# Layer 1 in another order on all five engines, attention values in 64x32 tiles, the last tile in halves of 256 columns, one masking pass moved

## The chip, the cores and the metric

The kernel runs on one core of a Trainium2 chip. A core has TensorE (matrix products into PSUM), VectorE, ScalarE, GpSimd and a DMA queue on SyncE; each takes its instructions in order, and they wait for each other by semaphores. All data are 32-bit floats. The metric is the device time of one execution in microseconds (us), lower is better. An fp32 matmul shows as two instructions in the trace, so 16 matmuls are 32 rows there.

## What is computed

A stack of two layers over x, 64 sequences of 32 rows with 512 columns. Layer 0 is a cross-attention over a context, self-attention and a linear layer with adapters. The change lies in layer 1 and in the gates ahead of it:

```python
# layer 1 of the reference, shortened
x = x + gates(layernorm(x), conv_w, gamma, beta)   # crucial and other channels, each scaled by a sigmoid gate
# attention: 8 heads of 32 columns, 32 rows per sequence, softmax over rows
q, k, v = split(layernorm(x) @ w_qkv.T + b_qkv)
scores = where(causal, k_h @ q_h.T, -10000.0)
attn = softmax(scores)
x = x + (attn @ v_h) @ w_o.T + b_o
x = x + layernorm(x) @ (W * mask).T
```

The gates need means and variances over all of x, so layer 1 can't begin before they are known.

## The kernel before

x lies in SBUF as 16 tiles (NT) of 128 rows (four sequences) by 512 columns, `x_tile(t)`. Four tiles are in flight; tile t uses lane u = t % 4 of the buffers and of PSUM, where `low(u)` and `high(u)` are two banks of 512 columns. Each tile goes through some 30 stages in layer 1. On TensorE: `turn_mix` (four 128x128 transposes of the gated features), `turn1` (of the normalised rows), `qkv` (16 matmuls of 128 columns for q and k, 4 of 256 for v), `scores`, `values`, `project`, `turn2`, `ffn` (4 matmuls of 512 columns). On ScalarE: `xnT1` and `xnT2` (copies of the turned rows), `evac_qk`, `exps`, `spread_p`, `evac_ot`. On GpSimd: `rstd1` and `rstd2` (the reciprocal root), `bias`, `spread_k`, `shift`. On VectorE: `gate`, `add_rest`, `mix`, `add_mix`, `stats1`, `rows1`, `evac_v`, `mask`, `turn_probs`, `add_proj`, `stats2`, `rows2`, `add_ffn`. On SyncE: `store`.

The order is set by numbers. `SLOTS1` gives each stage a place in the life of a tile, and `STARTS1` gives each of the first eight and the last four tiles its start. `over_lanes` sorts the stages of an engine by slot plus start; tiles in the middle follow in a loop, one tile per unit of the slots. Single entries can be overridden by `OPENING1` and `CLOSING1`. Before, TensorE and VectorE used `OPENING1`, ScalarE alone used `CLOSING1`. An engine never leaves its order: a stage that waits holds all behind it.

`values` computes for each of 8 heads the product of 128x32 of V with 128x128 of the spread probabilities. A tile holds four sequences, and each sequence attends only to itself, so `spread_p` writes the turned probabilities four times, each time with the rows of three sequences set to zero by a column of `jmask`.

In the gates, VectorE also multiplies the weights of the last product with their mask, in four passes (`mask_weights`, 128x512 each), between the short steps of the statistics. `keep_busy` issues matmuls on a constant that nothing reads: 13 stand ahead of the first `turn1`, 2 ahead of the projection of tile 14 and 7 ahead of the values of tile 15.

Of the kernel before, what the change touches and what calls it, by code (L numbers as in the profile page):

```python
# [64 lines left out]
def build_program(nc, a):  # L65
    ctx = ExitStack()
    with ctx:
# [3 lines left out]
        def sem(name):  # L71
# [12 lines left out]
            ("jmask", [P, TB]),  # L84
# [1106 lines left out]
def norm_turn(pe, n, t, u, xn, out, ident):  # L1191
    pe.wait_ge(n["xn"], t + 1)
    for c in range(DC):
# [16 lines left out]
    "gate": 0.000, "add_rest": 0.027, "mix": 0.173, "turn_mix": 0.485, "add_mix": 0.614, "stats1": 0.707,  # L1210
    "rstd1": 0.773, "rows1": 0.929, "bias": 2.020, "turn1": 1.011, "xnT1": 1.045, "qkv": 1.310,
    "evac_qk": 1.500, "evac_v": 1.762, "spread_k": 1.600, "scores": 2.006, "mask": 2.056, "shift": 2.136,
    "exps": 2.342, "turn_probs": 2.461, "spread_p": 2.571, "values": 2.919, "evac_ot": 2.919,
    "project": 3.015, "add_proj": 3.074, "stats2": 3.162, "rstd2": 3.245, "rows2": 3.395, "turn2": 3.470,
    "xnT2": 3.539, "ffn": 3.877, "add_ffn": 3.989, "store": 3.989,}
# [3 lines left out]
STARTS1 = ((0.00, 0.45, 0.99, 1.56, 3.50, 4.58, 5.35, 6.53),  # L1219
           (0.00, 37.47, 38.83, 39.38))  # L1220
# [3 lines left out]
OPENING1 = {("add_rest", 1): 0.715, ("mix", 1): 0.935, ("turn_mix", 1): 1.012}  # L1224
CLOSING1 = {("evac_ot", NT - 2): 41.65}
# [383 lines left out]
def mix_gates(nc, ctx, neghalf, ps, Y, ones, blend, band, affine, late, late_in, reduced):  # L1609
# [70 lines left out]
    def dve_program(dve):  # L1680
# [20 lines left out]
        mask_weights(2)  # L1701
# [18 lines left out]
def layer1(nc, ctx, a, X, mask, ident, neghalf, x_tile, ps, bufs, blend, early, late, late_in, ones, blended):  # L1720
# [32 lines left out]

    def sp_program(sp):
        def store(t, u):
            sp.wait_ge(s["ffn_added"], t + 1)
# [8 lines left out]
    def pool_program(pool):
# [308 lines left out]
```

## Time and profile before

| | |
|---|---|
| median of 3 runs | 2002.39 us (2001.21 to 2002.53) |
| the profiled execution, its own time | 2003.22 us |
| its span | 2001.3 us |
| layer 1 on TensorE, first turn to last matmul | 1761.37 to 1998.12 |
| TensorE, VectorE, ScalarE, GpSimd busy | 98%, 67%, 40%, 44% of the span |

Times in the rows count from the start of the span. A row of the timeline gives the start, the time from the first start to the last end of a group of like instructions, the engine (PE TensorE, DVE VectorE, ACT ScalarE, POOL GpSimd), the line, the tile written and the tiles read, and in brackets the idle time ahead of it and what ended it. The end of a matmul is modelled and takes in its drain, so successive groups on PE overlap a little: how long a stage holds TensorE is read from one start to the next.

### The profile page before, as it was taken

Reading aid. Unit: us, or ns where it says so; the run is one execution under the profiler, and the core shown is the slowest. Engines: PE = TensorE matmul, PEld = TensorE weight load, DVE = VectorE, ACT = ScalarE, POOL = GpSimd, SP = SyncE. Lnnn points to the kernel's source line nnn. Section 1 sums busy time; section 2 is a strip of 40 time slices with the busy share of each in tenths; the row PEclk is TensorE's granted clock in tenths of the full one; section 3 lists DMA queues with packets and bytes.
Section 4 is the critical chain, followed back from the end, with each engine's and each line's share of the span. In section 5 each row is a group of like instructions: output and inputs, shape, how many; then the busy total and the mean of one; then the engine's idle time right before and its main releaser. Section 6 shows DMA issues by size and latency. Waiting matters only on the chain. (4 is left out here: it accounts for less than half of the span.)

```text
span 2001.3 us, 41730 instructions
## 1 busy us (share of the span) xinstructions
PE 1963.2 (98%) x13298; PEld 1607.5 (80%) x13298; DVE 1332.3 (67%) x4426; ACT 802.4 (40%) x2285; POOL 883.1 (44%) x1506
## 2 busy tenths in 40 slices
PE   9999999999999999999999999999899999898998
PEld 7989889898988889898988989898665665575675
DVE  5846648483755748375574848466678888667875
ACT  3434435353444435344443544444333333232332
POOL 5543545354454536345453634446233333233442
PEclk9999999999999999999999999999999999999999
DMA  7100001010100101010010101010300000000000
GB/s 287 55 26 28 21 26 32 26 32 15 35 23 26 32 15 42 15 33 25 26 32 15 32 26 32 25 29 1 124 1 1 1 1 0 32 1 22 22 16 27
DMA packets 28323, 62.98 MB, mean 31 GB/s; under 512 B 14465, under 2 KB 15681, under 8 KB 27298
## 3 DMA queue, kind: packets, MB, share of 16 engines
q1 hardware_dynamic: 28194, 61.61, 9.4%
q8 instruction: 39, 0.64, 0.1%
q14 instruction: 90, 0.74, 0.1%
HBM read 54.15 MB, written 4.29 MB: 29 GB/s over the span
## 5 line engine op out<-in xcount | busy, mean ns | idle before, releaser
L792 ACT ACTIVATE probs<-psLane,nmax 128x289 f32<-128x289 f32 x256 | 126.7, 500 | 476.7 <-DVE nmax L914 476.7
L954 DVE MAX8 top<-work 128x8 f32<-128x257 f32 x512 | 180.1, 414 | 2.7
L492 PEld LDWEIGHTS psLane<-posT,lanes 128*128 128x128 f32 x1536 | 177.3, 192 | 4.8 <-ACT QT L781 0.6
L492 PE MATMUL psLane<-posT,lanes 128*128 128x128 f32 x1536 | 179.4, 275 | 0.4 <-ACT QT L781 0.4
L939 DVE TENSOR_TENSOR X<-X,psLane 128x512 f32 (+1 forms) x15 | 10.3, 687 | 242.0 <-PE psLane L1067 242.0
L1067 PE MATMUL psLane<-posT 128*128 128x512 f32 x384 | 167.7, 592 | 0.4 <-PEq L105 0.4
L767 ACT ACTIVATE w_o<-psLane 128x384 f32<-128x384 f32 (+1 forms) x256 | 113.9, 453 | 89.4 <-PE psLane L545 88.5
L345 POOL TENSOR_TENSOR tails<-probs,unit 128x66 f32<-128x66 f32 x128 | 38.1, 298 | 251.6 <-ACT probs L792 251.0
L565 PE MATMUL psLane<-KT,QT 96*128 96x289 f32 x512 | 146.0, 406 | 0.0
L1067 PEld LDWEIGHTS psLane<-posT 128*128 128x128 f32 x384 | 72.4, 190 | 84.9 <-issue 84.9
L370 POOL TENSOR_TENSOR KT<-w_qkv 128x128 f32<-128x128 f32 x64 | 29.2, 457 | 251.3 <-ACT w_qkv L739 251.3
L911 DVE TENSOR_REDUCE rmax<-psLane 128x2 f32<-128x578 f32 x128 | 97.0, 758 | 46.7 <-PE psLane L565 46.6
L515 PE MATMUL psLane<-hid,lanes 128*128 128x256 f32 x512 | 122.7, 381 | 0.0
L1173 POOL TENSOR_TENSOR lane_rstd<-lane_veps,neghalf 128x1 f32<-128x1 f32 x79 | 49.7, 629 | 161.8 <-DVE lane_veps L1168 161.8
L781 ACT ACTIVATE QT<-psLane 96x512 f32<-96x512 f32 x96 | 56.9, 593 | 131.9 <-PE psLane L492 131.3
L565 PEld LDWEIGHTS psLane<-KT,QT 96*128 96x128 f32 x512 | 91.2, 191 | 21.2 <-issue 7.2
L934 DVE COPY posT<-psLane 128x384 f32<-128x384 f32 x64 | 34.9, 545 | 104.4 <-PE psLane L621 104.4
L545 PE MATMUL psLane<-WvT,hid 128*128 128x192 f32 x512 | 104.2, 326 | 0.0
L545 PE MATMUL psLane<-w_ffn 128*128 128x192 f32 x512 | 104.1, 326 | 0.0
L958 DVE MATCH_REPLACE8 work<-top,work 128x257 f32<-128x257 f32 x256 | 102.3, 414 | 0.0
L958 DVE MATCH_REPLACE8 work<-top_last,work 128x257 f32<-128x257 f32 x256 | 102.2, 412 | 0.0
L958 DVE MATCH_REPLACE8 work<-top,hid 128x257 f32<-128x257 f32 x256 | 101.9, 408 | 0.0
(242 smaller groups left out, 5099.9 us busy)
## 6 DMA issues: line engine op xcount, KB each, us to landing
hid<-in_ctxT SPq DMA_DIRECT2D x64, 514.0 KB, 3.5
y<-X SPq DMA_DIRECT2D x16, 256.0 KB, 2.0
X<-in_x SPq DMA_DIRECT2D x1, 3584.0 KB, 21.1
lanes<-in_WqT SPq DMA_DIRECT2D x4, 768.0 KB, 9.6
Vtail<-Vlat SPq DMA_DIRECT2D x128, 24.0 KB
posT<-in_WoT SPq DMA_DIRECT2D x1, 3072.0 KB, 13.0
w_qkv<-in_w_qkv SPq DMA_DIRECT2D x2, 1536.0 KB, 6.9
w_ffn<-in_w_ffn SPq DMA_DIRECT2D x2, 1024.0 KB, 6.9
```

Source lines behind the costliest of these rows:

```text
L492: mm = pe.matmul(out[:, P * r:P * r + P], WqT[:, c, w:w + P], xnT[:, c, :], start=(c == 0), stop=(c == DC - 1))
L515: mm = pe.matmul(out[:, 0:MAIN], WkT[:, c, 2 * P:3 * P], hid[:, j, c, 0:MAIN], start=(c == 0), stop=(c == DC - 1))
L545: mm = pe.matmul(out, left(c), right(c), start=(c == 0), stop=(c == 1))
L565: mm = pe.matmul(psS[:, g % 2, 0:S], QT[:, g, j, :], KT[0:HD, j % 2, g, :], start=True, stop=True)
L767: act.activation(vproducts[:, 2 * f:2 * f + n, :].rearrange("p a n -> p (a n)"), psKV[:, kv_bank(t, 7 * j + 3 + f), 0:VH * n], ACT.Copy).t ...
L781: ins = act.activation(QT[at:at + hi - lo, g].rearrange("p j (r q) -> p r j q", r=G), src[lo:hi], ACT.Copy)
L792: act.activation(probs[:, g, :], psS[:, g % 2, 0:S], ACT.Exp, bias=nmax[:, g:g + 1], scale=XSCALE, accum_out=rsum[:, j % 2, g:g + 1]).then ...
L911: dve.tensor_reduce(rmax[:, 2 * h:2 * h + 2], psS[:, :, 0:S], AX.X, ALU.max).then_inc(rmax_done, 1)
L954: ins = dve.max(top[step // 2][:, c, :], src[:, c, :] if step == 1 else work[:, c, :])
L958: ins = dve.match_replace(work[:, c, :], picked[:, c, :], src[:, c, :] if step == 2 else work[:, c, :], GONE)
L1067: mm = pe.matmul(out, OT[:, n // G, n % G].rearrange("p j q -> p (j q)"), WoT[:, n, :], start=(n == 0), stop=(n == NKT * G - 1))
L1173: pool.tensor_tensor(small["rstd"][:, u], small["veps"][:, u], neghalf[:], ALU.pow).then_inc(n["rstd"], 1)
```

## The change

All numbers of `SLOTS1` and `STARTS1` are new, `OPENING1` grows from 3 entries to 24 and `CLOSING1` from 1 to 12, and all five engines now use both. `values` works on sequences in pairs: the two row halves of the array hold two sequences each, a matmul is 64 rows by 32 columns with 64 columns moving, and 16 of them replace 8; `spread_p` then writes two copies instead of four, with two new columns of `jmask`. For the last tile `xnT2`, `ffn`, `add_ffn` and `store` work on halves of 256 columns. In the gates `mask_weights(2)` stands ahead of the wait for the first sums instead of behind `moment`.

```diff
@@ SLOTS1, STARTS1, OPENING1, CLOSING1
-    "gate": 0.000, "add_rest": 0.027, "mix": 0.173, "turn_mix": 0.485, "add_mix": 0.614, "stats1": 0.707,
...
+    "gate": 0.0000, "add_rest": 0.3412, "mix": 0.4805, "add_mix": 0.5579, "stats1": 0.5919, "turn_mix": 0.7364,
...
-STARTS1 = ((0.00, 0.45, 0.99, 1.56, 3.50, 4.58, 5.35, 6.53),
-           (0.00, 37.47, 38.83, 39.38))
+STARTS1 = ((0.0000, 0.5197, 0.9241, 1.5710, 3.6120, 4.4460, 5.1756, 6.5717),
+           (0.0000, 34.2135, 38.2969, 38.6761))
@@ mix_gates, dve_program
+        mask_weights(2)
         dve.wait_ge(sums_done, 1)
         dve.tensor_scalar(minus_mean[:], sums, 1.0, None, ALU.mult).then_inc(mean_ready, 1)
         mask_weights(1)
         dve.wait_ge(sums_done, 2)
         dve.tensor_scalar(moment[:], sums2, -1.0, EPS, ALU.mult, ALU.add).then_inc(moment_ready, 1)
-        mask_weights(2)
@@ layer1
-    pT = lambda u: lanes[:, u, 1]
+    pT = lambda u: lanes[:, u, 1, 0:2 * EW].rearrange("p (h k q) -> p h k q", h=EH, k=2)
+    last_tile = lambda t: isinstance(t, int) and t == NT - 1
@@ store
+            if last_tile(t):
+                for n in range(2):
+                    sp.wait_ge(s["ffn_added"], t + 1 + n)
+                    sp.dma_start(a["y"][t][:, EW * n:EW * n + EW], x_tile(t)[:, EW * n:EW * n + EW]).then_inc(out_done, 16)
@@ every engine, here POOL
-        over_lanes(pool, SLOTS1, STARTS1, {
+        over_lanes(pool, SLOTS1, STARTS1, opening_slots=OPENING1, closing_slots=CLOSING1, stages={
@@ values
-            for h in range(EH):
-                n, at = h // 4, L * (h % 4)
-                mm = pe.matmul(high(u)[at:at + L, P * n:P * n + P], V[:, u, L * h:L * h + L],
-                               pT(u)[:, P * h:P * h + P], start=True, stop=True, tile_position=(0, at))
+            for n in range(2):
+                for c in range(EH // 2):
+                    for half in range(2):
+                        h, lo, at = 4 * n + c, 64 * half, 512 * half + 2 * L * n
+                        mm = pe.matmul(ps[L * c:L * c + L, u, at:at + 2 * L], V[lo:lo + 64, u, L * h:L * h + L],
+                                       pT(u)[lo:lo + 64, h].rearrange("p k q -> p (k q)"), start=True, stop=True,
+                                       tile_position=(lo, L * c))
@@ ffn
+            if last_tile(t):
+                for n, out in enumerate((low(u)[:, 0:EW], high(u)[:, 0:EW])):
+                    for c in range(DC):
+                        if (n, c) == (0, 2):
+                            pe.wait_ge(n5["xnT"], t + 2)
+                        mm = pe.matmul(out, xnT[:, u, c], w_ffn[:, c, EW * n:EW * n + EW], start=(c == 0), stop=(c == DC - 1))
+                    mm.then_inc(s["ffn_filled"], 1)
+                return
@@ spread_p
-            for j in range(TB):
-                ins = act.activation(pT(u).rearrange("p (h j q) -> p h j q", h=EH, j=TB)[:, :, j], v, ACT.Copy,
-                                     scale=jmask[:, j:j + 1])
+            for k in range(2):
+                ins = act.activation(pT(u)[:, :, k], v, ACT.Copy, scale=jmask[:, TB + k:TB + k + 1])
@@ xnT2 of the last tile
+            for n in range(2):
+                act.activation(xnT[:, u, 2 * n:2 * n + 2].rearrange("p c q -> p (c q)"), high(u)[:, EW * n:EW * n + EW],
+                               ACT.Copy).then_inc(n5["xnT"], 1)
@@ add_ffn
+            if last_tile(t):
+                for n, part in enumerate((low(u)[:, 0:EW], high(u)[:, 0:EW])):
+                    dve.wait_ge(s["ffn_filled"], t + 1 + n)
+                    half = x_tile(t)[:, EW * n:EW * n + EW]
+                    dve.tensor_tensor(half, half, part, ALU.add).then_inc(s["ffn_added"], 1)
+                return
```

TensorE's order, with names of tiles as out<-in. In the opening, from the scores of tile 1 on. Before (L1825 scores, L1194 turn1 or turn2, L1813 and L1817 qkv, L1840 values, L1848 project, L1854 ffn):

```order
L1825 MATMUL psLane<-lanes,w_ffn 32x128 x8
L1194 MATMUL psLane<-ident,lane_xn 128x128 x4
L1813 MATMUL psLane<-lane_xnT,w_qkv 128x128 x16
L1817 MATMUL psLane<-w_qkv,lane_xnT 128x256 x4
L1840 MATMUL psLane<-lanes,w_o 32x128 x8
L1825 MATMUL psLane<-lanes,w_ffn 32x128 x8
L1848 MATMUL psLane<-w_o,lane_xnT 128x512 x2
L1840 MATMUL psLane<-lanes,w_o 32x128 x8
L1848 MATMUL psLane<-w_o,lane_xnT 128x512 x2
L1194 MATMUL psLane<-ident,lane_xn 128x128 x4
```

The same place in the changed kernel, from turn1 of tile 3 on (L1840 is now scores, L1858 values, L1867 project, L1828 and L1832 qkv):

```order
L1194 MATMUL psLane<-ident,lane_xn 128x128 x4
L1840 MATMUL psLane<-lanes,w_ffn 32x128 x8
L1858 MATMUL psLane<-lanes,w_o 32x64 x16
L1840 MATMUL psLane<-lanes,w_ffn 32x128 x8
L1867 MATMUL psLane<-w_o,lane_xnT 128x512 x2
L1828 MATMUL psLane<-lane_xnT,w_qkv 128x128 x16
L1832 MATMUL psLane<-w_qkv,lane_xnT 128x256 x4
L1858 MATMUL psLane<-lanes,w_o 32x64 x16
L1867 MATMUL psLane<-w_o,lane_xnT 128x512 x2
L1194 MATMUL psLane<-ident,lane_xn 128x128 x4
```

The q/k/v product of tile 3 stood ahead of the values of tile 0, the scores of tile 2 and the projection of tile 0; now it stands behind them.

In the loop, from qkv to the next scores. Before:

```order
L1817 MATMUL psLane<-w_qkv,lane_xnT 128x256 x4
L1194 MATMUL psLane<-ident,lane_xn 128x128 x4
L1798 REGISTER_ALU
L1801 MATMUL psLane<-ident,lanes 128x128 x4
L1854 MATMUL psLane<-w_ffn,lane_xnT 128x512 x4
L1840 MATMUL psLane<-lanes,w_o 32x128 x8
L1825 MATMUL psLane<-lanes,w_ffn 32x128 x8
```

And in the changed kernel (L1816 is turn_mix, L1881 ffn):

```order
L1832 MATMUL psLane<-w_qkv,lane_xnT 128x256 x4
L1194 MATMUL psLane<-ident,lane_xn 128x128 x4
L1858 MATMUL psLane<-lanes,w_o 32x64 x16
L1813 REGISTER_ALU
L1816 MATMUL psLane<-ident,lanes 128x128 x4
L1881 MATMUL psLane<-w_ffn,lane_xnT 128x512 x4
L1840 MATMUL psLane<-lanes,w_ffn 32x128 x8
```

The values moved from behind the feed-forward product to ahead of the mix turn, and are thus needed one product and one turn earlier.

VectorE's order in the gates, from the partial sums on, before (L1682 is the masking pass, L1697 minus_mean, L1700 moment, L1703 scale):

```order
L1694 TENSOR_REDUCE part<-psLane 128x2 x4
L1697 TENSOR_SCALAR minus_mean<-psLane 128x2
L1682 TENSOR_TENSOR w_ffn<-w_ffn,ffn_mask 128x512
L1700 TENSOR_SCALAR moment<-psLane 128x2
L1682 TENSOR_TENSOR w_ffn<-w_ffn,ffn_mask 128x512
L1703 TENSOR_SCALAR mix_scale<-mix_rstd,affine 128x2
```

And in the changed kernel, with every line number higher by 10 or 11:

```order
L1704 TENSOR_REDUCE part<-psLane 128x2 x4
L1692 TENSOR_TENSOR w_ffn<-w_ffn,ffn_mask 128x512
L1708 TENSOR_SCALAR minus_mean<-psLane 128x2
L1692 TENSOR_TENSOR w_ffn<-w_ffn,ffn_mask 128x512
L1711 TENSOR_SCALAR moment<-psLane 128x2
L1713 TENSOR_SCALAR mix_scale<-mix_rstd,affine 128x2
```

No masking pass now runs while GpSimd computes the power between moment and scale.

## Rows read from the trace of the kernel before

**Rows 1.** The page: busy us (share of the span) and instructions.

```profile
PE 1963.2 (98%) x13298; PEld 1607.5 (80%) x13298; DVE 1332.3 (67%) x4426; ACT 802.4 (40%) x2285; POOL 883.1 (44%) x1506
```

**Rows 2.** Stretches of layer 1: start:end, us, busy time of each engine, clock.

```profile
1761.37:1820.37 59.00, 53.04 (x398) 39.02 (x399) 43.40 (x104) 18.44 (x48) 21.87 (x24) 0.97 0.03 10
1820.37:1860.93 40.56, 37.88 (x265) 26.33 (x264) 28.23 (x65) 11.23 (x29) 16.27 (x16) 1.00 0.06 21
1860.93:1969.00 108.07, 105.90 (x758) 74.85 (x757) 84.95 (x206) 37.98 (x96) 42.20 (x47) 1.00 0.05 20
1969.00:1998.12 29.12, 25.71 (x164) 15.24 (x162) 15.25 (x38) 7.92 (x19) 7.53 (x9) 1.00 0.05 19
```

**Rows 3.** Timeline of TensorE, one steady tile.

```profile
1874.45 3.73 PE L1813 MATMUL psLane<-lane_xnT,w_qkv 128*128 128x128 f32 x32
...
1879.75 0.60 PE L1194 MATMUL psLane<-ident,lane_xn 128*128 128x128 f32 x4
1880.19 0.60 PE L1801 MATMUL psLane<-ident,lanes 128*128 128x128 f32 x4
1881.04 3.70 PE L1854 MATMUL psLane<-w_ffn,lane_xnT 128*128 128x512 f32 x8 [0.25 <-ACT lane_xnT L1868]
1884.67 0.64 PE L1840 MATMUL psLane<-lanes,w_o 128*32 128x128 f32 x16
1885.13 0.62 PE L1825 MATMUL psLane<-lanes,w_ffn 128*32 128x128 f32 x16
1885.68 0.66 PE L1194 MATMUL psLane<-ident,lane_xn 128*128 128x128 f32 x4
1886.17 1.88 PE L1848 MATMUL psLane<-w_o,lane_xnT 128*128 128x512 f32 x4
1887.89 3.73 PE L1813 MATMUL psLane<-lane_xnT,w_qkv 128*128 128x128 f32 x32
```

**Rows 4.** Timeline of TensorE in the opening.

```profile
1761.86 4.69 PE L1606 MATMUL psLane<-ones 128*128 128x128 f32 x26
...
1789.56 3.84 PE L1813 MATMUL psLane<-lane_xnT,w_qkv 128*128 128x128 f32 x32 [1.14 <-ACT lane_xnT L1868]
...
1802.96 0.66 PE L1194 MATMUL psLane<-ident,lane_xn 128*128 128x128 f32 x4 [1.57 <-DVE lane_xn L1178]
...
1809.86 0.66 PE L1194 MATMUL psLane<-ident,lane_xn 128*128 128x128 f32 x4 [1.28 <-DVE lane_xn L1178]
...
1857.71 0.64 PE L1840 MATMUL psLane<-lanes,w_o 128*32 128x128 f32 x16
```

**Rows 5.** Timeline of VectorE in the opening.

```profile
1791.03 1.10 DVE L1964 TENSOR_TENSOR w_o<-w_o,lane_rinv 128x256 f32<-128x256 f32 x1
...
1796.20 0.42 DVE L1949 TENSOR_TENSOR w_o<-psLane,keep 128x256 f32<-128x256 f32 x1 [3.59 <-PE psLane L1825]
...
1801.43 1.47 DVE L1178 TENSOR_SCALAR lane_xn<-X,lane_mv,lane_rstd 128x512 f32<-128x512 f32 x1 [1.05 <-POOL lane_rstd L1173]
```

**Rows 6.** Timeline of TensorE, values and next scores in layer 0.

```profile
1575.66 1.16 PE L1404 MATMUL psLane<-lanes,lane_Vd 64*32 64x128 f32 x64
1576.75 1.16 PE L1385 MATMUL psLane<-lanes,lane_QT 64*128 64x128 f32 x16
```

**Rows 7.** Timelines of VectorE and GpSimd in and near the gates.

```profile
1753.08 0.16 DVE L1697 TENSOR_SCALAR minus_mean<-psLane 128x2 f32<-128x2 f32 x1 [1.15 <-PE psLane L1655]
...
1754.85 0.68 DVE L1682 TENSOR_TENSOR w_ffn<-w_ffn,ffn_mask 128x512 f32<-128x512 f32 x1
1755.01 1.08 POOL L1664 TENSOR_TENSOR mix_rstd<-moment,neghalf 128x2 f32<-128x2 f32 x1 [8.97 <-DVE moment L1700]
...
1741.03 0.55 POOL L1173 TENSOR_TENSOR lane_rstd<-lane_veps,neghalf 128x1 f32<-128x1 f32 x1 [1.81 <-DVE lane_veps L1168]
```

**Rows 8.** Timeline of ScalarE and VectorE in the closing.

```profile
1979.46 1.72 ACT L1888 ACTIVATE lanes<-lane_turned,jmask 128x256 f32<-128x256 f32 x4 [2.34 <-DVE lane_turned L1968]
...
1998.16 0.69 DVE L1977 TENSOR_TENSOR X<-X,psLane 128x512 f32<-128x512 f32 x1 [4.14 <-PE psLane L1854]
```

More of the change, by code:

```diff
@@ L83, in build_program @@
             ("block16", [P, 4]),
-            ("jmask", [P, TB]),
+            ("jmask", [P, TB + 2]),
             ("adapter", [LROWS, B]),
@@ L1209 @@
 SLOTS1 = {
-    "gate": 0.000, "add_rest": 0.027, "mix": 0.173, "turn_mix": 0.485, "add_mix": 0.614, "stats1": 0.707,
[L1211 to L1215, printed above, removed]
+    "gate": 0.0000, "add_rest": 0.3412, "mix": 0.4805, "add_mix": 0.5579, "stats1": 0.5919, "turn_mix": 0.7364,
+    "rstd1": 0.8470, "rows1": 0.8532, "xnT1": 1.0687, "turn1": 1.0916, "evac_qk": 1.4284, "qkv": 1.5586,
+    "spread_k": 1.7346, "evac_v": 1.9834, "scores": 2.0783, "mask": 2.1011, "exps": 2.1930, "turn_probs": 2.1947,
+    "shift": 2.3285, "spread_p": 2.3964, "bias": 2.4024, "evac_ot": 2.6574, "values": 2.7068, "project": 3.1126,
+    "add_proj": 3.1403, "stats2": 3.1597, "rows2": 3.3406, "rstd2": 3.4635, "xnT2": 3.5519, "turn2": 3.6348,
+    "add_ffn": 3.9352, "ffn": 3.9950, "store": 3.9950,}
 STARTS0 = ((0.0000, 0.9283, 1.9176, 2.9178, 3.9210, 4.9178, 5.9127, 6.9150),
            (0.0000, 125.1676, 126.4733, 127.2146))
-STARTS1 = ((0.00, 0.45, 0.99, 1.56, 3.50, 4.58, 5.35, 6.53),
-           (0.00, 37.47, 38.83, 39.38))
+STARTS1 = ((0.0000, 0.5197, 0.9241, 1.5710, 3.6120, 4.4460, 5.1756, 6.5717),
+           (0.0000, 34.2135, 38.2969, 38.6761))
 CLOSING0 = {
@@ L1223 @@
     ("reduce_rest", NT - 2): 131.0012, ("evac_pt", NT - 1): 128.7422, ("turn2", NT - 1): 129.9208,}
-OPENING1 = {("add_rest", 1): 0.715, ("mix", 1): 0.935, ("turn_mix", 1): 1.012}
-CLOSING1 = {("evac_ot", NT - 2): 41.65}
+OPENING1 = {
+    ("rows1", 0): 0.9598, ("rows2", 0): 3.5768, ("qkv", 1): 1.8863, ("stats2", 1): 3.7649, ("gate", 2): 1.0311,
+    ("mask", 2): 2.8893, ("turn_probs", 2): 3.2164, ("values", 2): 3.7087, ("add_ffn", 2): 5.1277,
+    ("turn1", 3): 2.5165, ("evac_qk", 3): 3.1253, ("spread_k", 3): 3.3705, ("rows2", 3): 4.9286,
+    ("add_ffn", 3): 5.7086, ("add_rest", 4): 3.7336, ("mix", 4): 3.9359, ("stats1", 4): 4.3771, ("qkv", 4): 5.4057,
+    ("rstd2", 4): 6.7559, ("xnT2", 4): 6.8586, ("ffn", 4): 7.4225, ("spread_p", 5): 6.8787,
+    ("turn_probs", 5): 7.0929, ("values", 5): 7.4584,}
+CLOSING1 = {
+    ("xnT2", NT - 3): 40.6522, ("turn2", NT - 3): 40.9440, ("ffn", NT - 3): 41.2903, ("add_ffn", NT - 3): 41.3164,
+    ("exps", NT - 2): 39.8485, ("spread_p", NT - 2): 40.5087, ("add_proj", NT - 2): 41.1058,
+    ("stats2", NT - 2): 41.2849, ("qkv", NT - 1): 40.5532, ("spread_k", NT - 1): 40.6372,
+    ("scores", NT - 1): 41.2134, ("values", NT - 1): 41.6104,}
 OPENING0 = {("rows3", 0): 3.7066,}
@@ L1760, in store @@
                 sp.dma_start(a["y"][bass.ds(t, 1)].rearrange("a p d -> (a p) d"), x_tile(t)).then_inc(out_done, 16)
-        over_lanes(sp, SLOTS1, STARTS1, {"store": store})
-        sp.wait_ge(out_done, 16 * NT)
+        over_lanes(sp, SLOTS1, STARTS1, opening_slots=OPENING1, closing_slots=CLOSING1, stages={"store": store})
+        sp.wait_ge(out_done, 16 * (NT + 1))
     def pool_program(pool):
@@ L1857, in pe_program @@
         pe.wait_ge(late_in, 16 * LATE_LOADS)
[L1858 removed]
+        over_lanes(pe, SLOTS1, STARTS1, opening_slots=OPENING1, closing_slots=CLOSING1, stages={
             "turn_mix": turn_mix, "turn1": turn1, "qkv": qkv,
```

24 lines of the change are left out of this document (16 added, 8 removed).

## The prediction

> **What bounds the kernel now.** I read the page first. TensorE is busy for 98% of the span [rows 1], so a change of this kernel can only pay where TensorE waits, or by making TensorE's own work shorter. All edits but one lie in layer 1, so the second view is the table of stretches from the first work of layer 1 (1761.37) to the end of its last matmul (1998.12) [rows 2]: TensorE is idle for 6.0 us in the first stretch, 2.7 in the second, 2.2 in the long steady one, 3.4 in the last. These idle times are too small, since the profile counts the drain of a matmul as busy. A better count is by starts.
>
> One steady tile [rows 3]: the q/k/v product takes 5.30 us from its start to the next start (1874.45 to 1879.75), each turn 0.44, the feed-forward product 3.63, the values 0.46 (1884.67 to 1885.13), the scores 0.55, a turn 0.49, the projection 1.72 (up to 1887.89). The period is 13.44 us. The only wait in it is 0.41 us: the second turn of 0.44 begins at 1880.19, so TensorE could go on at 1880.63, and goes on at 1881.04, when ScalarE has copied the turned rows. Outside the steady part I count the same way. From 1761.37 to 1860.93 (99.56 us) there are 21 turns (9.2), 7 q/k/v products (37.1), 7 scores at 0.55 (3.9), 6 values (2.8), 6 projections (10.3) and 5 feed-forward products (18.2): 81.5 us; the filler matmuls of the start, from 1761.86 on, take 4.5 until the first turn at 1766.39 [rows 4]. So TensorE waits 13.6 us in the opening.
>
> Where? In the timeline of the opening the marked waits are 1.14 us ahead of the fourth q/k/v product, 1.57 and 1.28 ahead of the turns of tiles 0 and 1 for the feed-forward [rows 4]. The cause stands on VectorE: it sits idle for 3.59 us until 1796.20, since it next needs the scores of tile 2, and these stand on TensorE behind the whole q/k/v product of tile 3 [rows 5]. After that VectorE is the engine that is behind, and TensorE waits for normalised rows.
>
> **The change, part by part.**
> *Opening order.* The new order puts scores 2 and projection 0 ahead of the q/k/v product of tile 3. VectorE gets its next mask about 4 us earlier and works through the product; TensorE doesn't wait for the turned rows of tile 3, which now have 2.7 us of other matmuls ahead of them. On ScalarE the q/k copy of tile 0 goes ahead of the xnT copy of tile 1, so GpSimd begins its spread earlier and the reciprocal root of tile 2 isn't held behind it. I followed the new order forward with the durations of the rows: VectorE 0.72 us for a 512-wide operation, 1.07 for statistics, 0.67 until the root is there, 1.35 for masking, 1.7 for normalising and turning probabilities; ScalarE 0.6 for xnT, 1.15 for q/k, now 0.9 for the spread; GpSimd 2.1 for its spread. In us after the first gate (1759.17 before), before and by this count: turn 2 of tile 0 43.8 and 39.9; of tile 1 50.7 and 46.8; end of the values of tile 5 99.0 (1857.71 plus 0.46) [rows 4] and 89.6. That is 9.4 us out of the 13.6. The count leaves out that VectorE and GpSimd get in each other's way: a normalising pass at 1791.03 took 1.10 us where 0.42 is usual, rows at 1801.43 took 1.47 in place of 0.55 [rows 5]; with two more of the kind the opening lost 3.6 us so. I charge the same again, since VectorE has no slack in that stretch. Gain 5.8; bounds 2.2 (twice the loss) and 9.4.
>
> *Steady order.* The values of a tile go between the turn and the mix turn ahead of the feed-forward product. From the start of the turn to the product now takes 1.29 us (1879.75 to 1881.04); with the values between, TensorE has 0.44 + 0.54 + 0.44 = 1.42 us of work there, and the wait of 0.41 is gone. The price is that the values' probabilities are needed 4.5 us earlier. VectorE's new order (mask, projection, statistics, probabilities at once, then rows) gives them at about 6.8 us after the scores, ScalarE spreads them until 7.7, and the values stand at 8.5: margin 0.8 us. What hides this step is that margin.
>
> *Values in 64x32 tiles.* 16 matmuls of 64 columns for 8 of 128, each two instructions in fp32. Before: 16 instructions in 0.46 us, 28.6 ns each. Layer 0 has the same tile with 128 columns: 64 instructions in 1.09 us, 17.0 ns each [rows 6]. No row has 64 columns. Below: half of 17.0 if columns alone count, 0.27 us a tile, 3.0 us less over 16 tiles. Above: 28.6 ns, 0.92 us, 7.4 more. I take 17.0, since the weight tile is the same one: 0.54 us, 0.08 more for each tile. ScalarE's spread falls from four passes to two, 1.72 [rows 8] to about 0.9 us, which counts only in the chains above.
> The Trainium skill speaks against this step: TensorE: Matmul & The Clock Gate, Back-to-back issue gap, gives a floor of about 25 ns for a matmul of 1 to 64 columns. The 17.0 ns of this trace lie below that floor, with tiles of the same shape, so I go by the row.
>
> *Gates.* The third masking pass now stands ahead of the wait for the sums, where VectorE is idle for 1.15 us [rows 7], and takes 0.68: hidden. Where it was, it began at 1754.85, and GpSimd's power, begun at 1755.01, took 1.08 us against 0.55 for the like one at 1741.03. Without it I expect 0.55, and all behind it 0.5 us earlier; TensorE has only filler there, so all of it counts. If the long power has another cause, the gain is 0.
> The Trainium skill, SBUF — State Buffer, two separate sides, says that VectorE and GpSimd share a pair of ports as an exclusive lock. By that rule the power waits for the pass; the trace agrees (0.53 us longer, and the pass ends at 1755.53).
>
> *Closing.* Followed in the same way from the end of the feed-forward product of tile 12, the new order ends its last product at 30.8 us against 32.0 (the values of tile 13 taken off): 1.2 gained, 0.25 of it by the half copy that lets the last product start after 256 columns. Behind it the last addition falls from 0.69 us [rows 8] to 0.42 (256 columns), and the last store has half the bytes: 0.4 together. The tuple of the filler (7 and 2) is unchanged, and about 1.5 us of filler still stands ahead of the last values.
>
> **The sum** against the profiled execution, 2003.22 us (span 2001.3 and 1.9 around it): opening -5.8; eight steady tiles at 0.41 less 0.08, -2.6; values of the other eight tiles +0.6; gates -0.5; closing -1.2; tail -0.4. That is -9.9, so 1993.3. The profiled execution is 0.83 above the median, 2002.39; I predict 1992.5.
>
> **The rivals.**
> *VectorE stays the bound of the opening.* For it: after 1796 it is nearly always busy, and operations that took 1.47 in place of 0.55 are frequent. Against: its idle 3.59 us is filled now. If the collisions double, the opening gives 2.2, and the time is 1996.1. Chance 16%.
> *The floor of 25 ns holds* for 64 columns: 32 instructions take 0.80 us, 0.26 more than I count, 4.2 us over 16 tiles, 1996.7. Against it the 17.0 ns of rows 6. Chance 6%. It is the rule of the Trainium skill that stands with the values above.
> *The steady part gets a new wait (slower).* The values wait for the spread probabilities, behind VectorE's chain mask, projection, statistics, probabilities. Each us by which that chain is later than its margin of 0.8 costs 8 us. It ends above 2002.4 from a delay of 2.0 us on: 1.2 a tile, 9.9 in all. For it: an operation of VectorE held by GpSimd loses 0.9, so three in a row would do. Against: in the new order the bias addition runs beside operations that read PSUM. At 2.2 us, 2004. Chance 6%.
> *Recovered waits return elsewhere.* What the opening gains is lost as TensorE runs into ScalarE or GpSimd later: within 0.2% of before. Chance 8%.
>
> **How the numbers follow.** My own case has 64%, with a range of 1988.5 (values at half price, 3.0, and a little more of the opening) to 1996. The whole range is 1988.5 to 1998.5, which takes in the first two rivals and most of the price of values at 28.6 ns. A measurement of this kernel can tell about 0.2%, 4 us, from no change; so faster means under 1998.4: 0.64 + 0.16 + 0.06 = 0.86; same 0.08; slower 0.06.
>
> **What would show it.** In the profile after: the values' group near 0.54 us from start to start; the mark of 3.59 on VectorE gone; turn 2 of tile 0 near 40 us after the first gate; a steady period near 13.1 us with no wait for ScalarE ahead of the feed-forward; the power at 0.55; the last addition at 0.42. I am wrong if the period stays at 13.4 or above, if values take over 0.8 us, or if TensorE's marks in the opening only move from one turn to another.

## The result, and the profile after

| | before | after |
|---|---|---|
| median | 2002.38 us | 1986.59 us (4 runs, 1985.97 to 1988.17) |
| profiled execution | 2003.22 us, span 2001.3 | 1985.98 us, span 1984.2 |

The ratio is 0.9923, with a 95% interval of 0.9912 to 0.9935: 15.8 us less. The forecast was 1992.5, 9.9 us less, with 1988.5 as the lower end of its range: the direction was right, the measured time lies 1.9 us below that end, and the gain is 1.6 times what was forecast. The sum had counted against the profiled execution; there the difference is 17.2 us.

The page, busy us, share of the span and instructions:

```profile
PE 1955.0 (99%) x13562; PEld 1605.6 (81%) x13562; DVE 1322.7 (67%) x4427; ACT 787.1 (40%) x2254; POOL 879.4 (44%) x1506
```

TensorE lost 8.2 us of busy time and the span 17.1, so by the page's count about half came out of idle time. Stretches of layer 1, from the first gate (1757.79 here, 1759.17 before) to the end of the values of tile 5, from there to the end of the last steady tile, and to the last matmul (start:end, us, busy time of each engine, granted clock):

```profile
1757.79:1846.34 88.55, 83.81 (x740) 62.33 (x738) 65.31 (x169) 25.27 (x65) 36.61 (x39) 1.00 0.04 13
1846.34:1950.66 104.32, 104.32 (x904) 73.64 (x898) 78.43 (x207) 30.98 (x81) 39.88 (x48) 1.00 0.06 21
1950.66:1981.60 30.94, 27.91 (x215) 18.31 (x213) 15.24 (x41) 6.68 (x17) 7.38 (x9) 1.00 0.08 29
```

The first row took 99.00 us before (1759.17 to 1858.17) and takes 88.55. In the second TensorE has no idle time left; before, the steady stretch had 2.2 us [rows 2].

The timeline of TensorE, one steady tile (start, time, engine, line, tiles, and in brackets the idle time and what ended it), to be held against [rows 3]:

```profile
1862.21 3.73 PE L1828 MATMUL psLane<-lane_xnT,w_qkv 128*128 128x128 f32 x32
...
1867.51 0.60 PE L1194 MATMUL psLane<-ident,lane_xn 128*128 128x128 f32 x4
1868.04 0.45 PE L1858 MATMUL psLane<-lanes,w_o 64*32 64x64 f32 x32
1868.42 0.66 PE L1816 MATMUL psLane<-ident,lanes 128*128 128x128 f32 x4
1868.91 3.60 PE L1881 MATMUL psLane<-w_ffn,lane_xnT 128*128 128x512 f32 x8
1872.44 0.64 PE L1840 MATMUL psLane<-lanes,w_ffn 128*32 128x128 f32 x16
1873.02 0.66 PE L1194 MATMUL psLane<-ident,lane_xn 128*128 128x128 f32 x4
1873.51 1.88 PE L1867 MATMUL psLane<-w_o,lane_xnT 128*128 128x512 f32 x4
1875.23 3.73 PE L1828 MATMUL psLane<-lane_xnT,w_qkv 128*128 128x128 f32 x32
```

No row has a mark of idle time. From start to start: q/k/v 5.30 us, turn 0.53, values 0.38, mix turn 0.49, feed-forward 3.53, scores 0.58, turn 0.49, projection 1.72: a period of 13.02 here, and 13.04 on average from the values of tile 6 to those of tile 13. Counted the same way the kernel before has 13.48 (13.44 in the tile of rows 3); the forecast was 13.11. The values' 32 instructions take 0.38 us, 11.9 ns each. The feed-forward product takes 3.53 where it took 3.63 behind its wait.

ScalarE in the same tile:

```profile
1865.89 0.91 ACT L1915 ACTIVATE lanes<-lane_turned,jmask 128x256 f32<-128x256 f32 x2 [2.35 <-DVE lane_turned L2006]
1866.70 1.12 ACT L1902 ACTIVATE w_ffn<-psLane,b_qk 128x128 f32<-128x128 f32 x4
1868.14 0.60 ACT L1895 ACTIVATE lane_xnT<-psLane 128x512 f32<-128x512 f32 x1 [0.32 <-PE psLane L1194]
```

The spread takes 0.91 us [1.72 in rows 8], the q/k copy follows, and ScalarE then waits 0.32 us for TensorE's turn: now TensorE is the one that is waited for.

The opening, TensorE:

```profile
1760.48 3.07 PE L1616 MATMUL psLane<-ones 128*128 128x128 f32 x26
1764.15 0.66 PE L1194 MATMUL psLane<-ident,lane_xn 128*128 128x128 f32 x4 [0.60 <-DVE lane_xn L1178]
...
1786.42 0.64 PE L1840 MATMUL psLane<-lanes,w_ffn 128*32 128x128 f32 x16 [0.32 <-POOL lanes L1788]
1787.00 1.98 PE L1867 MATMUL psLane<-w_o,lane_xnT 128*128 128x512 f32 x4
1788.82 3.73 PE L1828 MATMUL psLane<-lane_xnT,w_qkv 128*128 128x128 f32 x32
...
1795.23 1.98 PE L1867 MATMUL psLane<-w_o,lane_xnT 128*128 128x512 f32 x4 [0.56 <-ACT lane_xnT L1920]
1797.25 0.66 PE L1194 MATMUL psLane<-ident,lane_xn 128*128 128x128 f32 x4
...
1804.05 0.60 PE L1194 MATMUL psLane<-ident,lane_xn 128*128 128x128 f32 x4
```

The marks of 1.14, 1.57 and 1.28 us [rows 4] are gone. The two last rows are the turns for the feed-forward of tiles 0 and 1: 39.46 and 46.26 us after the first gate, where the count by hand had 39.9 and 46.8. The filler of 26 instructions took 4.69 us before [rows 4] and takes 3.07; the first turn stands 6.36 us after the first gate, before 7.22.

VectorE in the opening, the normalising passes that answer to the long ones of [rows 5]:

```profile
1793.78 0.42 DVE L2002 TENSOR_TENSOR w_o<-w_o,lane_rinv 128x256 f32<-128x256 f32 x1
...
1796.65 0.55 DVE L1178 TENSOR_SCALAR lane_xn<-X,lane_mv,lane_rstd 128x512 f32<-128x512 f32 x1 [1.65 <-POOL lane_rstd L1173]
```

And all normalising passes of rows in the first stretch of after (count, busy us, mean ns of one, idle before):

```profile
L1178 DVE TENSOR_SCALAR lane_xn<-X,lane_mv,lane_rstd 128x512 f32<-128x512 f32 x13 | 7.3, 561 | 4.2 <-POOL lane_rstd L1173 4.1
```

The same 13 took 854 ns each before. Up to the second turn of tile 1, VectorE's operations were 4.35 us longer than usual before (six of them; the prediction counted four, 3.6 us); after, none is. GpSimd's own operations are lengthened in both: by 1.6 us in before and by 1.65 in after over the same stretch, five of them each time (a root of 0.93 us in place of 0.55, for one). So the two engines still seem to meet in the new order, and GpSimd is the one that loses time.

The gates and the end, VectorE and GpSimd:

```profile
1752.09 0.16 DVE L1708 TENSOR_SCALAR minus_mean<-psLane 128x2 f32<-128x2 f32 x1 [0.55 <-PE psLane L1665]
...
1754.02 0.70 POOL L1674 TENSOR_TENSOR mix_rstd<-moment,neghalf 128x2 f32<-128x2 f32 x1 [9.01 <-DVE moment L1711]
...
1979.97 0.42 DVE L2019 TENSOR_TENSOR X<-X,psLane 128x256 f32<-128x256 f32 x1 [2.29 <-PE psLane L1877]
1981.62 0.42 DVE L2019 TENSOR_TENSOR X<-X,psLane 128x256 f32<-128x256 f32 x1 [1.24 <-PE psLane L1877]
```

The pass fills the idle time ahead of minus_mean (1.15 to 0.55) and the power takes 0.70 us instead of 1.08 [rows 7]. The last addition is 0.42.

Where the 17.1 us of the span went, by landmarks of the two timelines: first gate 1.4 earlier; opening, first gate to the end of the values of tile 5, 99.0 to 88.55, 10.4; from there to the feed-forward product of tile 12, 103.8 to 100.8, 3.0; closing, from there to the last matmul, 36.2 to 34.5, 1.7; behind it 3.17 to 2.59, 0.6.

### The profile page after: what moved, and what is told of

It reads as the page before. It is cut to its first block and busy times, and to the rows that moved or that the text cites. A ratio compares the mean times of both kernels' runs of the same rounds, so it can differ in the third digit from the quotient of the medians.

```text
span 1984.2 us, 42231 instructions
## 1 busy us (share of the span) xinstructions
PE 1955.0 (99%) x13562; PEld 1605.6 (81%) x13562; DVE 1322.7 (67%) x4427; ACT 787.1 (40%) x2254; POOL 879.4 (44%) x1506
## 5 line engine op out<-in xcount | busy, mean ns | idle before, releaser
L1067 PEld LDWEIGHTS psLane<-posT 128*128 128x128 f32 x384 | 72.4, 190 | 84.9 <-issue 84.9
L1173 POOL TENSOR_TENSOR lane_rstd<-lane_veps,neghalf 128x1 f32<-128x1 f32 x79 | 46.8, 592 | 139.2 <-DVE lane_veps L1168 138.7
## 6 DMA issues: line engine op xcount, KB each, us to landing
posT<-in_WoT SPq DMA_DIRECT2D x1, 3072.0 KB, 13.2
```

Of the source, the lines that this page charges most:

```text
L1067: mm = pe.matmul(out, OT[:, n // G, n % G].rearrange("p j q -> p (j q)"), WoT[:, n, :], start=(n == 0), stop=(n == NKT * G - 1))
```

## The experiments

Two questions: why the opening gained all that the count by hand gave, and on which part of the change the steady gain hangs. The theory: the steps of the forecast hold, and two of their sizes were wrong, the charge for VectorE and GpSimd in each other's way, and the price of the values. The rivals: the gain comes from the single move of the q/k/v product of tile 3; from fewer ScalarE passes rather than from matmuls; or from filler that ran at another clock. Letters in the expectations hold for their own run. All medians are in us, ratios are to the kernel before, which ran beside each of them at 2002.38 to 2002.78. The executions of one kernel lie up to 5 us apart, so differences of 1 or 2 us between medians are read from the traces instead, as the time from the first gate to the last matmul ("layer 1" below).

| run | median | ratio | interval |
|---|---|---|---|
| e1_order_only | 1991.75 | 0.9943 | 0.9929 to 0.9956 |
| e2_parts_only | 2000.59 | 0.9991 | 0.9981 to 1.0000 |
| e3_opening_only | 1994.27 | 0.9956 | 0.9943 to 0.9970 |
| e4_qkv3_later | 2004.49 | 1.0014 | 1.0005 to 1.0023 |
| e5_values_twice | 1991.75 | 0.9945 | 0.9927 to 0.9964 |
| e7_pool_old | 2001.08 | 0.9997 | 0.9988 to 1.0006 |
| e8_filler8 | 2003.09 | 1.0010 | 1.0000 to 1.0019 |
| e9_spread_twice | 1991.22 | 0.9941 | 0.9928 to 0.9954 |
| e10_old_values | 1993.12 | 0.9950 | 0.9937 to 0.9963 |
| e11_qkv3_spread2 | 2003.49 | 1.0005 | 0.9996 to 1.0013 |
| e12_no_end_filler | 1985.91 | 0.9915 | 0.9902 to 0.9928 |
| e13_pool_old_spread2 | 1995.23 | 0.9965 | 0.9953 to 0.9978 |

### Order alone, parts alone

```diff
@@ e1_order_only: before, with all four new tables on all five engines
@@ e2_parts_only: after, with the four old tables
```

> The kernel before with the new order alone (all tables, all five engines); values in 128x32 tiles, last tile whole, masking pass where it was. Theory A, the order carries nearly all: opening about 9 us shorter from the first gate to the values of tile 5, the steady period 13.1 us (13.44 before), closing 1 us shorter, so 1989 to 1991. Theory B, the parts (two spread passes for four, cheaper values) carry a third or more: 1993 to 1997.

> The changed kernel with the order of before in all tables. Theory A: only the gates (0.4), the first filler (0 to 0.9), the last tile (0.8) and a shorter spread ahead of a few values (0.5): 1999.5 to 2001. Theory B: 1995 to 1998. By the rule of 25 ns for a matmul of up to 64 columns values would take 0.80 us a tile and it would be slower than before by 2 or more; I expect 0.38 as in the changed kernel.

The order alone gives 10.6 us, the parts alone 1.8, both 15.8: 3.4 us come only when they are together. The intervals of these medians are some 2 us and more to each side; the periods show the same thing more clearly: 13.48 before, 13.39 in e1, 13.45 in e2, 13.04 after, so 0.32 us a tile, 2.6 us over eight tiles, come only with both. e1 lies between the ranges of its two theories: A is right on the opening and wrong on the period (13.1). e2 lies in that of A. In e1 the opening is as short as after (feed-forward product of tile 4 at 84.9 us after the first gate; 84.5 after, 94.9 before). So the order shortens the opening, and by itself hardly shortens the steady tile. The timeline of ScalarE in a steady tile of e1 shows what holds there:

```profile
1882.06 1.71 ACT L1898 ACTIVATE lanes<-lane_turned,jmask 128x256 f32<-128x256 f32 x4 [2.35 <-DVE lane_turned L1978]
1883.67 1.11 ACT L1885 ACTIVATE w_ffn<-psLane,b_qk 128x128 f32<-128x128 f32 x4
1884.67 0.60 ACT L1878 ACTIVATE lane_xnT<-psLane 128x512 f32<-128x512 f32 x1
```

The spread of four passes pushes the q/k copy, and that the xnT copy for which the feed-forward product waits. There is no idle mark between the three, and the last ends at 1885.27. TensorE is no earlier: its group of values holds it for 0.58 us in this place (0.46 in rows 3, 0.38 after), and its mix turn, begun at 1884.79, takes 0.49. Both engines are done within 0.05 us of each other, and the product starts at 1885.33. From the turn to the product it is 1.65 us, 1.40 after.

### The opening alone

```diff
@@ over_lanes: e3_opening_only
+    if slots is SLOTS1:
+        slot1 = [SLOTS1N[name] for name in stages]     # ...N: the new tables
+        first = sorted((OPENING1N.get((names[n], t), STARTS1N[0][t] + x), t, n) for n, x in enumerate(slot1)
+                       for t in range(2 * LANES) if t + x < 2 * LANES)
```

> The kernel before with the new order in the opening alone (everything up to the loop); loop and closing in the old order. Theory A: 8.5 to 9.5 us faster, 1993 to 1994, and no operation of VectorE held by GpSimd before the turn of tile 3. My prediction's term (5.8): 1996.6.

It gained 8.1 us of the median and 9.0 of the profiled executions, near theory A; the feed-forward product of tile 4 stands at 85.8 (94.9 before), the rest of the layer is as before (period 13.48). VectorE's long operations are gone here too, with the former values and four spread passes: up to the second turn of tile 1 none is longer than usual. GpSimd's operations are 1.66 us longer than usual, as in before. The opening is the largest part of the gain, and belongs to the order.

### One move of it alone

```diff
@@ e4_qkv3_later
-OPENING1 = {("add_rest", 1): 0.715,
+OPENING1 = {("qkv", 3): 3.20, ("evac_qk", 3): 3.34, ("add_rest", 1): 0.715,
@@ e11_qkv3_spread2: the same, and
+            ("spread_k", 2): 2.40,
```

> The kernel before with one product moved: q/k/v of tile 3 on TensorE behind projection 0, and its copy on ScalarE behind exps of tile 2. If VectorE's idle time of 3.59 us behind the scores of tile 2 is the cause of the opening's waits, this alone gives about half of the opening, 3 to 4 us: 1998.5 to 1999.5. If the cause is spread over all the reordered stages, under 1 us.

> e4 with one more move: GpSimd's spread of k for tile 2 ahead of bias and shift of tile 1. In e4 the scores of tile 2 waited 2.29 us for that spread, which stood behind a shift that waited for the mask of tile 1, and the projection behind it ran at half clock. If that is what spoiled e4, the wait and the slow projection go, and the kernel is 3 to 5 us faster than e4 (2004.5): 1999.5 to 2001.5. If the moved product is of no use in itself, it stays above 2002.

Neither gave the gain that was expected: e4 is 2.1 us slower than before, and e11 no different from it. In e4 TensorE has the scores of tile 2 ahead of the q/k/v product, but they wait for GpSimd, which spreads their keys behind the shift of tile 1:

```profile
1790.85 1.02 PE L1825 MATMUL psLane<-lanes,w_ffn 128*32 128x128 f32 x16 [2.29 <-POOL lanes L1773]
1791.80 3.25 PE L1848 MATMUL psLane<-w_o,lane_xnT 128*128 128x512 f32 x4
```

The projection behind the wait takes 3.25 us where 1.88 is usual [rows 3]; over these two the granted clock is 0.58. In e11 that wait is gone, and the next one stands there: the projection waits 1.97 us for ScalarE's copy, which is queued behind the exponentials of tile 1, and a low clock follows. VectorE's operations are 2.9 us longer than usual there. This move on TensorE gained nothing while the engines that feed it kept their order; that it's of no use in itself isn't shown.

### GpSimd's order

```diff
@@ over_lanes: e7_pool_old (after)
+    if slots is SLOTS1 and "bias" in names:            # GpSimd only
+        slot1 = [SLOTS1N[name] for name in stages]     # ...N: the former tables
+        first = sorted((OPENING1N.get((names[n], t), STARTS1N[0][t] + x), t, n) for n, x in enumerate(slot1)
+                       for t in range(2 * LANES) if t + x < 2 * LANES)
@@ e13_pool_old_spread2: the same, and
+OPENING1N = {("spread_k", 2): 2.40, ("add_rest", 1): 0.715, ...
```

> The changed kernel with GpSimd's order of before in the opening (bias ahead of shift and so on); loop and closing as in the changed kernel. Theory A, the new order on GpSimd is what keeps its operations out of VectorE's way: rows of 1.4 and more return on VectorE, 2 to 4 us slower than the changed kernel, 1989 to 1990.5. Theory B, VectorE had slack for them and only the order on TensorE counts: under 1 us slower.

The miss is in size (theory A had 2 to 4 us): with the former order on GpSimd alone, and only in the opening, 14.5 of the 15.8 us are gone. GpSimd of after, then of e7:

```profile
1784.24 2.04 POOL L1788 TENSOR_TENSOR lanes<-w_ffn,jmask 128x512 f32<-128x512 f32 x2 [1.58 <-ACT w_ffn L1902]
1787.20 0.62 POOL L1796 TENSOR_TENSOR w_o<-w_o,lane_rmax 128x256 f32<-128x256 f32 x1 [0.93 <-DVE lane_rmax L1992]
```

```profile
1788.15 0.61 POOL L1812 TENSOR_TENSOR w_o<-w_o,lane_rmax 128x256 f32<-128x256 f32 x1 [3.96 <-DVE lane_rmax L2008]
1788.72 2.04 POOL L1804 TENSOR_TENSOR lanes<-w_ffn,jmask 128x512 f32<-128x512 f32 x2
```

In e7 GpSimd sits idle 3.96 us for the shift of tile 1 while the spread of the keys of tile 2, begun at 1784.24 in after, stands behind it. TensorE, and two of VectorE's operations:

```profile
1790.90 1.08 PE L1856 MATMUL psLane<-lanes,w_ffn 128*32 128x128 f32 x16 [3.85 <-POOL lanes L1804]
1791.91 3.78 PE L1883 MATMUL psLane<-w_o,lane_xnT 128*128 128x512 f32 x4
1795.49 4.45 PE L1844 MATMUL psLane<-lane_xnT,w_qkv 128*128 128x128 f32 x32
```

```profile
1782.92 1.54 DVE L2018 TENSOR_TENSOR w_o<-w_o,lane_rinv 128x256 f32<-128x256 f32 x1
...
1803.78 1.48 DVE L1178 TENSOR_SCALAR lane_xn<-X,lane_mv,lane_rstd 128x512 f32<-128x512 f32 x1 [1.65 <-POOL lane_rstd L1173]
```

The wait of 3.85 is followed by 4.59 us at a granted clock of 0.50, the 1.2 GHz level (start:end, us, busy times, clock), and the projection's time doubles:

```profile
1790.90:1795.49 4.59, 4.59 (x21) 2.14 (x21) 2.18 (x6) 1.32 (x3) 1.89 (x2) 0.50 0.00 0
```

VectorE's excess is back: 3.96 us in the stretch where after has none. At 1782.92 GpSimd begins its bias addition of 1.27 us in the same hundredth. And there is a second long wait of TensorE, 3.64 us ahead of the first turn of tile 5 (1834.48), with a granted clock of 0.62 in the 4.5 us behind it.

> The changed kernel with GpSimd in its former order of the opening lost 14.5 us: the scores of tile 2 waited 3.85 us for the spread of their keys, TensorE then ran 4.6 us at a granted clock of 0.50, and VectorE lost 3.96 us in operations held by GpSimd. This run keeps that former order but for one step: the spread of the keys of tile 2 stands ahead of the bias and the shift of tile 1. Theory A, the late keys cost most: the wait of 3.85 goes, with the low clock behind it, the q/k/v product of tile 3 starts near 32 us after the first gate (37.7 there, 31.0 in the changed kernel), and the median is 1989 to 1993. Theory B, the holds of VectorE cost most: of the five long operations four stay (2.9 of the 3.96 us, since the one at 1782.92 stood beside the bias that moves), and the median stays at 1996 or above.

One step moved on GpSimd brings 5.9 us back, with the wait and the low clock behind it (q/k/v of tile 3 at 31.0, as after); 8.6 stay. The median lies between what A and B gave, so neither is the whole. In layer 1 it is 238.9 us in e7, 230.7 in e13 and 223.8 after: 6.9 us stay. VectorE's excess is still 3.78 us, and the turn of tile 0 waits 1.58 and that of tile 1 1.07 for VectorE's rows; by the q/k/v product of tile 4 e13 is 3.1 us behind after. By that of tile 5 it is 6.9 behind, and what lies between is the second long wait of e7, unchanged. It is again a matter of one queue: GpSimd's root for the first rows of tile 5, whose input is there at 1820.96, stands behind the spread of the keys of tile 4, so VectorE is idle for 4.79 us and TensorE for 3.64:

```profile
1824.37 2.04 POOL L1804 TENSOR_TENSOR lanes<-w_ffn,jmask 128x512 f32<-128x512 f32 x2 [6.71 <-ACT w_ffn L1918]
1826.37 0.55 POOL L1173 TENSOR_TENSOR lane_rstd<-lane_veps,neghalf 128x1 f32<-128x1 f32 x1
1828.48 0.66 PE L1194 MATMUL psLane<-ident,lane_xn 128*128 128x128 f32 x4 [3.64 <-DVE lane_xn L1178]
```

After has them the other way round (root at 1817.47, spread at 1820.80), and no wait. The rows behind the late root are held too (1.48 us for 0.55), which is 0.9 of the 3.64. So the holds can account for the 3.1 and the 0.9, some 4 us, at most; the rest of what the former order costs is waits behind one queue, and the low clock that followed them in e7. What a hold costs by itself no run takes apart.

### The values and their spread

```diff
@@ e5_values_twice
-            for n in range(2):
+            for n in (0, 1, 0, 1):
@@ e9_spread_twice
+            extra = lanes[:, u, 1, 2 * EW:4 * EW].rearrange("p (h k q) -> p h k q", h=EH, k=2)
+            for dst in (extra, pT(u)):
@@ e10_old_values: after, with the values in 128x32 tiles and four spread passes
```

> The changed kernel with each group of 16 value matmuls issued twice, same operands and same result. What the matmuls of 64 columns take on TensorE stands then in the period: 0.38 us a tile if they run at 11.9 ns an instruction, as the changed kernel's timeline shows (16 tiles: 6.1 us, so 1992.7); 0.54 at 17.0 ns, the price that I predicted (8.7, 1995.3); 0.80 by the rule of 25 ns (12.8, 1999.4).

> The changed kernel with ScalarE writing its two copies of the probabilities a second time, to columns that nothing reads: ScalarE as long as in the kernel before (1.72 us a tile), TensorE's values short. Theory A, the loop is shorter than with the order alone because ScalarE is free sooner for its q/k and xnT copies: the period rises from 13.04 to about 13.3, 1989 to 1990. Theory B, it is the shorter matmuls: period 13.05 to 13.1, 1986.6 to 1987.5.

> The changed kernel with values in 128x32 tiles and four spread passes again; new order, halves of the last tile and gates kept. With the order alone at 1991.75 and the changed kernel at 1986.59, the halves and the gates give 0.4 and 0.8 to 1.2, so 1990.2 to 1990.8 if the rest of the difference, 3.5 to 4 us, is that of the values' form; 1987 to 1988 if it is not.

The doubled values cost 5.2 us over 16 tiles (5.0 in layer 1; 6.1 was expected at 11.9 ns, the lowest of the three prices), and stand in the timeline as 64 instructions in 0.79 us, 12.3 ns each; the period is 13.44:

```profile
1884.16 0.86 PE L1858 MATMUL psLane<-lanes,w_o 64*32 64x64 f32 x64
1884.95 0.66 PE L1816 MATMUL psLane<-ident,lanes 128*128 128x128 f32 x4
```

e9 leaves the matmuls short and only makes ScalarE's spread as long as before; e10 has both long. Periods 13.39 and 13.40, medians 4.6 and 6.5 us above after, both more than was expected. The five executions of e10 lie between 1989.28 and 1994.16, and its layer 1 is 4.0 us longer than after, so its 6.5 is no good measure; the layer 1 of e9 is 5.2 us longer, 1.3 more than that of e10, and all of the 1.3 stands behind the feed-forward product of tile 13, where e9 has a granted clock of 0.68 behind a wait of 1.81 us and e10 1.00 behind the same wait. ScalarE in e9:

```profile
1880.22 1.71 ACT L1917 ACTIVATE lanes<-lane_turned,jmask 128x256 f32<-128x256 f32 x4 [2.35 <-DVE lane_turned L2008]
1881.84 1.11 ACT L1902 ACTIVATE w_ffn<-psLane,b_qk 128x128 f32<-128x128 f32 x4
1882.84 0.60 ACT L1895 ACTIVATE lane_xnT<-psLane 128x512 f32<-128x512 f32 x1
```

It is the picture of e1. Two chains run side by side from the turn to the feed-forward product: TensorE's turn, values and mix turn, and ScalarE's spread, q/k copy and xnT copy. With ScalarE's chain alone as long as before it is 13.39, with both long 13.40, and only with both short 13.04. TensorE's chain alone was made longer than it ever was in before (e5, 0.79 us of values, 13.44); the values of before with the short spread were not run. The tile of e1 in which no wait stands is an estimate for them: 1.60 us from the turn to the product, where it is 1.40 after, so 13.2 to 13.3. That is why order and parts gain more together: the new order puts the values and their spread into this place, and short values and a short spread make the place fit.

### The filler

```diff
@@ e8_filler8 (before)
-        busy_until_first(t, 13)
+        busy_until_first(t, 8)
@@ e12_no_end_filler (after)
-busy_at_end(t, (2, 0))   busy_at_end(t, (0, 7))
+busy_at_end(t, (0, 0))   busy_at_end(t, (0, 0))
```

> The kernel before with 8 filler matmuls in place of 13 ahead of the first turn of layer 1. In the profile of before the filler ran at half clock and ended 0.9 us after the rows were there. Theory A: the first turn comes 6.3 us after the first gate whatever the clock, 0.9 us less where it was 7.2, 2001.5 to 2002. Theory B: the lower activity lets the clock fall under the products behind it and costs 1 us or more.

> The changed kernel without the filler matmuls of the last two tiles (2 and 7). In its profile the probabilities of tile 15 are spread at 1966.96, the projection ahead of the filler ends at 1967.47, and the values begin at 1969.13. Theory A, the filler itself is the wait: 1.3 to 1.8 us faster, 1984.8 to 1985.3. Theory B, without it the clock falls to half under the last products: slower by 1 us or more, with a granted clock below 1 in the last stretches.

e8: in its profiled execution the first turn stands at 6.36 us after the first gate instead of 7.22, and the last matmul ends at 238.1 instead of 239.0; the median does not show it (2003.09, spread 6 us), so it is inconclusive. The clock of the filler goes with an edit of the change all the same. In before the 4.53 us from the filler to the first turn had a granted clock of 0.62, and after 1.00 in the like stretch. Ahead of both, TensorE waits for the first mix turn, in before and then in after:

```profile
1761.37 0.66 PE L1801 MATMUL psLane<-ident,lanes 128*128 128x128 f32 x4 [2.06 <-DVE lanes L1919]
1759.98 0.66 PE L1816 MATMUL psLane<-ident,lanes 128*128 128x128 f32 x4 [1.68 <-DVE lanes L1957]
```

The wait is 0.38 us shorter, as much as the power behind the moved masking pass gave. All eight profiles with that move have a wait of 1.68, a filler of 3.07 us and the first turn at 6.36; of the five without it and with 13 matmuls of filler, four have 2.06, a filler of 4.3 to 4.7 us and 7.22, and e1 has 2.06 and yet 3.07 and 6.36. So the 0.86 us come most likely with the moved pass; no run moves the pass alone.

e12: the last matmul ends 222.2 us after the first gate instead of 223.8, with no low clock; the median is 0.7 us below after, within the spread of both. It is the version with the lowest median, but not shown to be faster than after.

## Why the prediction was right in direction and short in size

**Right.** *The count by hand.* It gave 9.4 us for the opening. Measured: 10.4 to the end of the values of tile 5, of which 0.86 is filler ahead of the first turn, so 9.6; the two turns came within 0.6 us of their forecast, and VectorE's mark of 3.59 is gone. *The steady order.* The wait of 0.41 is gone and nothing took its place; the values wait for nothing in the steady tile. *Closing*: 1.2 forecast, 1.7 measured less the 0.46 of a values stage that now stands elsewhere, so about 1.3. *Tail*: 0.4 and 0.58. *Gates*: the power fell by 0.38 (0.70 in after, e2, e5 and e7; 1.08 in e1 and e3, which lack the move), 0.5 was forecast; it didn't fall to the 0.55 of the like one, which has one column to its two, and no run shows whether that is the reason. The first gate is 1.4 us earlier, but it stands between 1757.8 and 1760.1 in runs with the same code up to it, so the other 1.0 can't be told from that spread.

**The step that failed: "I charge the same again".** The opening was put down at 5.8, 9.4 by the count less 3.6 for VectorE and GpSimd in each other's way, "since VectorE has no slack in that stretch". The charge was nought: no operation of VectorE is held in that stretch of after, and the count without the charge, 9.4, was met by the 9.6 measured. The holds are not a rate that goes with how busy VectorE is; they go with the order: 4.35 us in before, 4.1 in e4, 4.4 in e2 and 2.9 in e11, with GpSimd's former order or nearly so; none in e1, e3 and after, with the new one; 3.96 in e7, which puts GpSimd's former order of the opening back and nothing else. The prediction followed the stages of VectorE forward, but not what GpSimd does beside each of them, though both orders could be read. The Trainium skill, SBUF — State Buffer, two separate sides, says that GpSimd and those operations of VectorE that need the shared pair of ports (two inputs from SBUF, or its faster mode) lock it for a whole instruction, whichever starts first; e7 agrees (1.54 us for 0.42 beside an addition of 1.27 that began at the same time). In after it is GpSimd whose operations are longer, by 1.65 us in all. The order decides who meets whom, and who waits.

**Mis-sized: the values.** 17.0 ns an instruction were taken from 128 columns in layer 0; with 64 columns it is 11.9, 0.38 us a tile in place of 0.54. The term was +0.6 for eight tiles and is -0.6; in the steady tiles a further 0.16 each is set off by longer turns (0.53 and 0.49 where 0.44 was counted), and the feed-forward product gives 0.10 when no wait stands ahead of it, so the period is 13.04 and not 13.11. That the forecast came so near is luck in part: values counted 0.16 too long and turns 0.14 too short cancel. The rival of 25 ns is refuted by e5 and by the trace. The Trainium skill, TensorE: Matmul & The Clock Gate, Back-to-back issue gap, gives that floor for a matmul by itself; its TensorEngine Tiling (Array Packing), Available Configurations and Key Properties, lists 64x32 as eight tiles that work independently, and instructions at 11.9 ns agree with tiles of the two row halves that overlap, which no run here takes apart.

**Not counted: ScalarE's half.** "Which counts only in the chains above" was too little. Without the short spread the steady wait comes back in another place (e9, period 13.39), 4.6 us in all. And the values' form was put at 0.08 us a tile, while in the new place it is 0.20 (0.58 in e1, 0.38 after). So the loss of 0.41 per tile was taken out only by the order, the short spread and the short values together. The forecast had the period nearly right with the short spread in its numbers; it gave the cause to TensorE's order alone.

**Not forecast: the filler's clock**, 0.86 us ahead of the first turn in this pair of profiles, most likely a second gain of the moved masking pass. The prediction said that TensorE has only filler there, and left out at which clock it runs.

**The range.** Its lower end took the values at half price and only a little more of the opening. The prediction's own bounds, 9.4 for the opening and 0.27 us for the values of 16 tiles, together give 1984.6, which takes in the 1986.59.

By stretch, forecast and measured: gates 0.5 and 1.4; opening 5.8 and 10.4; from there to the feed-forward product of tile 12, 2.6 less 0.6 and 3.0; closing 1.2 and 1.7; tail 0.4 and 0.6. Of the 7.3 us that were missing between the two profiled executions (5.9 between the medians) the opening alone makes 4.6, and the charge 3.6 of these.

## What to carry to other kernels

Follow a new order forward on every engine, and beside each operation of VectorE read what GpSimd runs: a hold goes with the pair of orders, and is not a tax to be charged again. When a stage is moved next to another, look for the second chain that ends at the same place: here both had to be short. And a move on the engine that waits may be worth nothing until those that feed it are moved as well: one queue left in its former order took back 14.5 us of 15.8, most of it in two places where one step stood behind another that wasn't ready.

## What the runs showed of the hardware beyond what was expected

A wait of TensorE of some 2 us or more in the opening could cost nearly as much again behind it: after 3.85 us of waiting the clock stood at 0.50 for 4.59 us (e7), which cost 3.1 us in three products, and after 2.29 at 0.58 for 4.03 (e4), 1.8 us. The waits of 1.14, 1.57 and 1.28 us in before had a clock of 1.00 behind them. But the length of the wait alone doesn't decide it: the same wait of 3.64 us ahead of the first turn of tile 5 had a clock of 0.62 behind it in e7 and of 1.00 in e13, and one of 1.81 us ahead of the values of tile 14 a clock of 0.68 in e9 and of 1.00 in e10.

Matmuls of 64 columns in 64x32 tiles run at 11.9 ns an instruction in fp32, 128 columns with the like tile at 17.0 and with 128x32 tiles at 28.6: half the columns do not give half the time. A product of 512 columns takes 3.53 us when TensorE comes to it without a pause, 3.63 behind a pause of 0.25.
